# Softmax denominators divided once per batch, and a step table for each engine, in a transformer block on one core

## What is computed

```python
x = layernorm(x + attn(x))
logits = x @ router_w + router_b
probs = softmax(logits); top_p, top_i = top_k(probs, 2); top_p /= top_p.sum(-1)
h = silu(x @ w1[e]) * (x @ w3[e])          # for each expert e
x = layernorm(x + sum_e gates[:, e] * (h @ w2[e]))
```

## Time and profile before

| | us |
|---|---|
| median of three runs | 432.3 |
| profiled execution | 429.85 |
| its span | 428.1 |
| TensorE busy in the span | 374.9 (88%) |
| VectorE busy | 327.2 (76%) |
| ScalarE busy | 246.9 (58%) |
| GpSimd busy | 205.8 (48%) |
| a steady attention stage, 174.5 to 199.0 | 24.5 |
| end of attention, first expert matmul | 247.64 |
| last matmul | 421.68 |

### The profile page before, as it was taken

One profiled execution on the slowest core, in us unless ns is written; L12 is line 12 of the kernel. 1 busy time (PEld: TensorE's weight loads), 2 busy tenths in 40 slices (PEclk: granted clock), 3 DMA queues, 4 the chain that ended last, 5 costly groups with the idle time before them and its releaser, 6 DMA issues.

```text
span 428.1 us, 7151 instructions
## 1 busy us (share of the span) xinstructions
PE 374.9 (88%) x2276; PEld 190.4 (44%) x2298; DVE 327.2 (76%) x973; ACT 246.9 (58%) x347; POOL 205.8 (48%) x267
## 2 busy tenths in 40 slices
PE   7879799997999999999997896888878889789993
PEld 3432222322233232323223265676657666567881
DVE  4878998997999999998995526656884687565655
ACT  2454177776878787877875853454345434445560
POOL 6067688515244251434433143545464555446771
PEclk9996889999999999999998998999999999999997
DMA  6762014483332433243011040000200020003000
GB/s 224 232 174 48 1 23 100 144 260 59 91 83 47 103 76 93 52 112 57 11 17 25 3 125 0 0 0 3 98 24 2 0 100 26 0 1 100 25 1 25
DMA packets 49635, 27.44 MB, mean 64 GB/s; under 512 B 31227, under 2 KB 45243, under 8 KB 49598
## 3 DMA queue, kind: packets, MB, share of 16 engines
q1 hardware_dynamic: 46702, 25.09, 22.5%
q10 hardware_dynamic: 2896, 1.90, 1.5%
HBM read 17.31 MB, written 7.38 MB: 58 GB/s over the span
## 4 chain that ended last, share of the span: by engine, by line
PE 52%; DVE 20%; issue 12%; ACT 6%; POOL 6%; DMA 2%; ACTq 0%; POOLq 0%; DVEq 0%; SPq 0%
PE o_bank L1254 12%; PE bank L1213 9%; PE t_bank L1236 7%; PE bank L1318 6%; PE t_bank L1318 5%; PE t_bank L1331 5%; PE small_bank L1213 4%; POOL hid_lo L680 4%; DVE maxima L962 3%; DVE den_all L1018 3%; DVE num L1090 3%; DVE x_tw L958 3%; ACT num L836 3%; ACT num L777 2%; DVE mg_t L958 2%
## 5 line engine op out<-in xcount | busy, mean ns | idle before, releaser
L777 ACT ACTIVATE num<-t_bank 128x1024 f32<-128x1024 f32 (+2 forms) x160 | 141.9, 943 | 61.8 <-PE t_bank L1236 61.7
L680 POOL TENSOR_TENSOR hid_lo<-num,q_op 128x512 fp32r<-128x512 f32 x63 | 86.2, 1373 | 67.7 <-ACT q_op L829 67.1
L650 POOL TENSOR_SCALAR_AFFINE_SELECT num<-num 128x512 f32<-128x512 f32 x64 | 40.2, 638 | 96.0 <-ACT num L777 94.4
L1254 PE MATMUL o_bank<-num,v_op 128*32 128x512 f32 (+3 forms) x768 | 79.6, 501 | 0.9
L829 ACT ACTIVATE q_op<-num 128x512 fp32r<-128x512 f32 x64 | 40.4, 632 | 65.0 <-DVE num L1090 64.3
L1213 PE MATMUL bank<-k_op,q_op 128*128 128x512 bf16 (+7 forms) x232 | 67.2, 338 | 2.5 <-DVE maxima L958 1.2
L962 DVE TENSOR_REDUCE maxima<-bank 128x1 f32<-128x512 f32 x90 | 59.8, 685 | 3.1 <-PE bank L1213 2.7
L1236 PE MATMUL t_bank<-q_op,k_op 64*128 64x512 bf16 (+3 forms) x384 | 49.4, 334 | 4.9 <-DMA q_op<-max_rows 2.2
L1090 DVE TENSOR_TENSOR num<-bank,num 128x512 f32<-128x512 f32 x32 | 22.1, 691 | 38.7 <-ACT num L836 32.4
L1213 PEld LDWEIGHTS bank<-k_op,q_op 128*128 128x128 bf16 x254 | 21.0, 97 | 57.9 <-DVE maxima L958 20.0
L958 DVE CUSTOM_DVE_ANT_0 x_tw<-bank,resid 128x256 f32<-128x256 f32 (+7 forms) x100 | 43.2, 454 | 4.4 <-PE bank L1213 3.5
(11 more groups left out here) (150 smaller groups left out, 604.6 us busy)
## 6 DMA issues: line engine op xcount, KB each, us to landing
q_op<-q_scratch SPq DMA_DIRECT2D x64, 48.0 KB
k_op<-k_scratch SPq DMA_DIRECT2D x32, 96.0 KB, 2.3
w_raw<-in_w_all SPq DMA_DIRECT2D x6, 512.0 KB, 4.6
turns_sb<-gate_scratch SPq DMA_DIRECT2D x8, 256.0 KB, 3.7
num<-gate_scratch SPq DMA_DIRECT2D x8, 256.0 KB, 3.8
xT<-o_sb SPq DMA_DIRECT2D x32, 32.0 KB
den_all<-o_sb SPq DMA_DIRECT2D x32, 32.0 KB
x_res<-in_x_tok ACTq DMA_DIRECT2D x4, 256.0 KB, 3.0
```

The costliest lines, as they stand in the source:

```text
L650: pool.affine_select(out=tile, in_=tile, compare_op=ALU.is_ge, fill=0.0, base=0, pattern=[[0, GH], [1, P]], channel_multiplier=-1)\
L680: pool.tensor_tensor(hid_lo[:, m % HB, :], hid[:, m % HB, :], hid_hi[:, m % HB, :].bitcast(F32), ALU.subtract).then_inc(f_lo, 1)
L777: act.activation(num[:, t % PB, :, off:CH].rearrange("p (k i) t -> p i k t", i=2)[:, :, h:h + each, :], t_bank[k % TB][:, :, 0:each * (CH ...
L1254: ins = pe.matmul(o_bank[h * QD:(h + 1) * QD, off:CH], v_op[w][:, kt, h, :], num[:, t % PB, h, off:CH], start=kt == 0, stop=kt == TI * (c ...
```

## The change

**Denominators.** Of the eight equal rows of a head only one is taken, and it goes to memory: `gather_heads` issues four transfers of sums and one of four rows of `o_sb`, [4 x 1024], to `den_scratch`. When a batch's four groups are there, `load_den` loads its 16 x 1024 denominators as a tile of 128 x 128, VectorE takes the reciprocal in place (`turn_den`), `store_rden` stores it, and `spread_rden` loads it into `rden_all` with each head's row in eight partitions. For batch 0 these stand, on SP, in the stage of group 5 (load, behind the weights and the gathering), in the last steady stage (store behind the gathering, spread at its end), and on VectorE at the head of the last steady stage; for batch 1 on SP behind the last gathering, and on VectorE behind unit 9 of chunk 0. Front step r = 0 is the product alone. ScalarE's copy of a group waits for the transfers of two groups before, and now for the denominators' too.

**Steps.** The rule r + 3 gives way to a table per engine. Before, r stood at step r + 3 everywhere; after:

| engine | r: step |
|---|---|
| TensorE | 1: 3, 6: 10, 8: 13, 14: 18 |
| VectorE | 0: 1, 1: 3, 2: 4, 3: 5, 5: 8, 7: 11, 9: 13, 10: 14, 11: 15, 13: 17, 14: 18 |
| ScalarE | 7: 11, 8: 12, 12: 16 |
| GpSimd | 3: 6 |

(TensorE's matmuls of r = 1 stood at step 4 before, since its work for the front steps has its own numbers: 1, 6, 8, 14.) The gates' product of an expert and its sum, both in unit 6 + 4e before, stand in units 6 + 4e and 7 + 4e. The transposes behind the last unit move from step 19 to 21, the statistics from 20 to 21 and 22 in halves, the variance from 21 to 23, 1/sqrt to 24, the output from 22 to 25. ScalarE does a unit's copies and Silus first, those of the older chunk behind those of the newer, and a front step last.

```diff
-TR_STEP = EO_STEP + UNITS - FT + 1
-STAT_STEP = TR_STEP + 1
-VAR_STEP = RSTD_STEP = STAT_STEP + 1
-Z_STEP = VAR_STEP + 1
+TR_STEP = EO_STEP + UNITS - FT + 3
+STAT_STEP = TR_STEP
+VAR_STEP = STAT_STEP + 2
+RSTD_STEP = VAR_STEP + 1
+Z_STEP = RSTD_STEP + 1
+RDEN_STEP = 9
...
-NEXT_AT = E_LAST
-def next_steps(n, i):
-    r = n - NEXT_AT
-    return [(i + 1 + r // UNITS, r % UNITS)] if i + 1 + r // UNITS < CHUNKS else []
+PE_NEXT = {1: 3, 6: 10, 8: 13, 14: 18}
+DVE_NEXT = {0: 1, 1: 3, 2: 4, 3: 5, 5: 8, 7: 11, 9: 13, 10: 14, 11: 15, 13: 17, 14: 18}
+ACT_NEXT = {7: 11, 8: 12, 12: 16}
+POOL_NEXT = {3: 6}
+def next_steps(n, i, table):
+    at = i * UNITS + n
+    return [(ch, r) for ch in range(1, CHUNKS) for r, step in table.items() if (ch - 1) * UNITS + step == at]
...
                 for h in range(GH):
-                    for k, dst in enumerate((o_all, den_all)):
-                        at, rows = g * QD + h * DH, h * QD + k * DH
-                        sp.dma_start(dst[at:at + DH, b * S:(b + 1) * S], o_sb[n % 2][rows:rows + DH, :])\
-                            .then_inc(heads_in[b][n % 2], 16)
+                    at = g * QD + h * DH
+                    sp.dma_start(o_all[at:at + DH, b * S:(b + 1) * S], o_sb[n % 2][h * QD:h * QD + DH, :])\
+                        .then_inc(heads_in[b][n % 2], 16)
+                sp.dma_start(den_dram[b, g * GH:(g + 1) * GH, :], o_sb[n % 2][DH:P:QD, :])\
+                    .then_inc(den_stored[b][n % 2], 16)
+            def load_den(b):
+                for i in range(2):
+                    sp.wait_ge(den_stored[b][i], 16 * (NG // 2))
+                sp.dma_start(den_sb[:, b, :], den_dram[b, :, :].rearrange("h (k t) -> (h k) t", t=P))\
+                    .then_inc(den_loaded[b], 16)
+            def store_rden(b):
+                sp.wait_ge(den_turned[b], 1)
+                sp.dma_start(rden_dram[b, :, :].rearrange("h (k t) -> (h k) t", t=P), den_sb[:, b, :])\
+                    .then_inc(rden_stored[b], 16)
+            def spread_rden(b):
+                sp.wait_ge(rden_stored[b], 16)
+                sp.dma_start(rden_all[:, b * S:(b + 1) * S], rden_dram[b, :, :].unsqueeze(1).broadcast_to([H, DH, S]))\
+                    .then_inc(rden_loaded[b], 16)
...
                         if step == ("T", 1, TI, 0, 0):
                             gather_heads(n - 1)
+                            if s == GROUPS - 1:
+                                store_rden(0)
+                        if step == ("END",) and s == GROUPS - 1:
+                            spread_rden(0)
...
+                        if n == NG + 1:
+                            load_den(0)
...
                 if ch == 0:
                     gather_heads(GROUPS - 1)
+                    load_den(B - 1)
+                    store_rden(B - 1)
+                    spread_rden(B - 1)
...
+                            act.wait_ge(den_stored[(g - 2) // NG][g % 2], 16 * ((g - 2) % NG // 2 + 1))
...
-                steps = next_steps(n, i)
-                for ch, r in steps:
-                    if r == 1:
-                        between(ch, ch // NC, ch % NC, r)
-                experts_hi(i, n)
                 if n >= UNITS:
                     experts_hi(i + 1, n - UNITS)
-                for ch, r in steps:
-                    if r != 1:
-                        between(ch, ch // NC, ch % NC, r)
+                experts_hi(i, n)
                 experts_silu(i, n)
                 if n >= UNITS:
                     experts_silu(i + 1, n - UNITS)
+                for ch, r in next_steps(n, i, ACT_NEXT):
+                    between(ch, ch // NC, ch % NC, r)
...
+            def turn_den(b):
+                dve.wait_ge(den_loaded[b], 16)
+                dve.reciprocal(den_sb[:, b, :], den_sb[:, b, :]).then_inc(den_turned[b], 1)
...
-                    dve.reciprocal(den_all[:, at], den_all[:, at]).then_inc(c_mg, 1)
-                    dve.wait_ge(c_mg, ch + 1)
-                    dve.tensor_tensor(mg_t[:, :], o_all[:, at], den_all[:, at], ALU.mult).then_inc(c_mgs, 1)
+                    dve.tensor_tensor(mg_t[:, :], o_all[:, at], rden_all[:, at], ALU.mult).then_inc(c_mgs, 1)
...
+                if n > EO_STEP and (n - EO_STEP) % FT == 1 and n < EO_STEP + 1 + UNITS:
+                    e = (n - EO_STEP) // FT
                     for k, half in enumerate(halves(ch, e)):
                         dve.wait_ge(f_eo, 2 + ch * E + e + 1 + k)
...
-                if n == STAT_STEP:
-                    for i in range(TI):
+                if n in (STAT_STEP, STAT_STEP + 1):
+                    for i in range(TI // 2 * (n - STAT_STEP), TI // 2 * (n - STAT_STEP + 1)):
...
+                if (ch, n) == (0, RDEN_STEP):
+                    turn_den(B - 1)
```

More of the change, by code:

```diff
@@ L367, in transformer_block @@
         heads_in = [[sem(f"heads_in{b}{i}") for i in range(2)] for b in range(B)]
+        den_stored = [[sem(f"den_stored{b}{i}") for i in range(2)] for b in range(B)]
+        den_loaded, den_turned, rden_stored, rden_loaded = ([sem(f"{n}{b}") for b in range(B)] for n in (
+            "den_loaded", "den_turned", "rden_stored", "rden_loaded"))
         max_split, max_joined, split_step, ident_cast = sem("max_split"), sem("max_joined"), sem("split_step"), sem("ident_cast")
@@ L688, in _ @@
                 experts(0, n)
-                for step in next_steps(n, 0):
+                for step in next_steps(n, 0, POOL_NEXT):
                     between(*step)
@@ L695, in _ @@
                     experts(i, n)
-                    for step in next_steps(n, i):
+                    for step in next_steps(n, i, POOL_NEXT):
                         between(*step)
@@ L979, in stage @@
                         experts(0, step[1])
+                        for next_step in next_steps(step[1], 0, DVE_NEXT):
+                            between(*next_step)
             for s in range(GROUPS):
@@ L1133, in _ @@
                 experts(0, n)
-                for step in next_steps(n, 0):
+                for step in next_steps(n, 0, DVE_NEXT):
                     between(*step)
@@ L1140, in _ @@
                     experts(i, n)
-                    for step in next_steps(n, i):
+                    for step in next_steps(n, i, DVE_NEXT):
                         between(*step)
@@ L1350, in _ @@
                 experts(0, n)
-                for step in next_steps(n, 0):
+                for step in next_steps(n, 0, PE_NEXT):
                     between(*step)
@@ L1357, in _ @@
                     experts(i, n)
-                    for step in next_steps(n, i):
+                    for step in next_steps(n, i, PE_NEXT):
                         between(*step)
```

13 lines of the change are left out of this document (9 added, 4 removed).

## The result

The changed kernel takes 401.2 us in the median of four runs (401.1 to 402.81), the kernel before 432.28 (431.94 to 432.59) beside it. The ratio is 0.929, interval 0.9265 to 0.9314: faster, and inside the range. The profiled execution of after took 401.1 us with a span of 399.4, where before had 429.85 and 428.1. So 28.7 us of span have to be found.

What follows compares the result with a forecast made beforehand. TensorE should be full but waits 7.7 us per chunk for VectorE's work or a ScalarE copy. 3.0 + 9.8 + 17.8 - 0.4 - 0.3 = 29.9 us off 429.85 gives 399.95, median 402.4 us, range 397.5 to 412.

Steps and rivals of the forecast that it cites:

- Sum: Whole kernel: savings of 29.9 us off the profiled 429.85 us give 399.95, and a median of 402.4 us.
- The 2.45: Whole kernel: the median was taken to lie 2.45 us above the profiled run.
- part 3: Last attention stage: wait of 1.62 us for mg_t goes, plus 0.75 and some 0.8 of slow clock; 3.0 us, bounds 1.6 to 3.4.
- Part 1: Divisions on VectorE: 128x128 per batch at 0.85 us instead of 3.34 us per chunk; the second costs nothing.
- The 0.3 of loss: Last steady stage: the first division, beyond 0.64 us of VectorE idle time, may push the score ring; bounds 0 and 0.9.
- Part 2: Denominators through memory: spread lands between 221 and 224.5, hidden with 1 to 3 us of cover; at the far end costs 1 us.
- SP is freed by 2 us per group: SP's queue: each group issues five transfers instead of eight at 0.7 us each.
- Part 4: Expert chunks: the table spreads VectorE's work; waits at small pieces go, stops cost 0.5 us per chunk, bounds 0 and 2.
- L999 1.3 to 3.0: Step 8 of a chunk on VectorE: four x1 operations take 1.3 to 3.0 us together beside GpSimd's remainders.
- Rival (a): Expert chunks: the shared lock holds VectorE's sums, 1.3 us more in four steps, 9 us in three chunks, 411 us; chance 0.10.
- Rival (b): Expert chunks: waits move, the projection waiting for gates_t behind the router; only the divisions' share is left, 421 us; chance 0.12.
- Rival (c): Attention stages: ScalarE's copies wait for the denominators' store if it takes over 30 us; 33 us lost, 435; chance 0.03.

Runs made afterwards that it cites:

- e3: Changed kernel with three extra SP transfers behind the denominators of group 0 (402.47 us) or of each of groups 1 to 7 (401.18 us).
- after_again: The changed kernel itself, untouched, timed once more on another chip: 399.43 us, ratio 0.9256 to the kernel before.
- e5_again: Changed kernel with the steps from x1's transposes through the router one unit earlier, timed a second time: 397.5 us, ratio 0.9212 to the kernel before.
- e2: Changed kernel with the new step table but the old denominators (eight transfers per group, division of 512 columns in each chunk): 416.35 us, ratio 0.9613 to before.
- e1: Kernel before with the denominators' path through memory and one division per batch, steps as before: 422.77 us, ratio 0.9765 to before.

## Why the prediction was right, step by step

- **Sum.** 29.9 us were forecast off the profiled run, 28.7 came (399.95 against 401.1), and the median then lay 0.1 above the profiled run, not 2.45. Two misses of 1.2 and 2.35 with opposite signs give 402.4 against 401.2; that part of the closeness is luck. The 2.45 may have been the clock's: where before was timed again, the mean granted clock of an execution lay between 0.956 and 0.973 and its time between 435.68 and 428.45, longer mostly where the clock was lower. After's four runs all had 0.972. And the range's low end doesn't add up as stated: 3.4 in part 3, no stops and no loss give 397.75 from the 399.95 of the profiled run, but 400.2 from the forecast of 402.4.
- **Part 1, divisions at 0.85 us.** L979 took 0.95 at 195.78 and 0.94 in chunk 0, and the idle time of 0.64 behind the first is gone. The score ring lost nothing: the starts of the mask part in that stage and the one before (172.89, 197.43) lie 24.54 us apart, as in before. The 0.3 of loss came all the same, 0.29 in the next stage (24.94 against 24.65), but by GpSimd's cast that VectorE's product held, which the forecast didn't have. The size is right by luck.
- **Part 2, path through memory.** The spread left SP at 213.57 and the page gives 4.4 us to landing, so 218.0, earlier than 221; mg_t was made at 220.62 and nobody waited. Right, with more cover than stated. "SP is freed by 2 us per group" was right as a size and wrong as a price: it was 2.2 us at group 0. The step that failed is that I looked for who stood behind the three new transfers and not for who stood behind the three removed. e3 shows it.
- **Part 3, last attention stage 3.0 us.** The 1.62 came. The 0.75 and 0.8 of the slow clock didn't: I read "after that idle time" as a cause, from one trace. after_again and e5_again, equal in code and idle time, show that the idle time before it doesn't decide it. In after_again, without the stretch, A is 5.06 shorter than before's: 2.2 early and 2.8 here, near my 3.0. So whether part 3 comes out is a matter of the execution. In after A shrank by 3.93, 2.2 of it early and 1.7 here, below my 3.0 and just above my lower bound of 1.6. In 1.7, the 0.29 of part 1 is taken off.
- **Part 4, chunks.** 9.8 + 17.8 - 0.4 = 27.2 forecast, 8.88 + 7.65 + 8.18 = 24.7 measured. The mechanism was right, and no wait is left at the four small pieces. Mis-sized was the full chunk, 36.25 against 37.53. The stop took 1.27 and not 0.5: 0.75 of idle time and 0.5 by which the units before and behind it are slower, which a row of idle time doesn't show. The other 0.5 is small work: the unit behind each small piece takes 2.16 (304.48 to 306.64) and not 2.07, and the one transpose of gates 0.26 behind a stop (283.59 to 285.92 is 2.33), 0.08 without one, where I had 0.1.
- **"L999 1.3 to 3.0."** The four x1 operations of a chunk took 1.10 us and were not held by a remainder. Instead small operations of the router got 1.2 to 1.4 us each, which the forecast knew from one row, the 1.27 of L1063. The lateness landed in step 15, as forecast, with other owners.
- **Rival (a)**, the lock on the sums, didn't come: sums took 0.68 to 0.80 us. The lock turned on VectorE all the same, on operations of 16 to 64 columns, for 1.27 us a chunk instead of 3. **Rival (b)**'s wait before the projection came where the division stayed, in e2, and not in after. **Rival (c)**: nothing waited for the store.

## What to carry to other kernels

When a queue is made shorter, look for the transfer with the least time behind each removed entry, as one does for an added one; three transfers of 21 more mattered here. A table of steps pays even where one operation is longer than the slack between two of the repeated ones (14.9 us with the division of 3.3 us in place), but each such operation leaves a stop, here 3.07 us. Before you call two parts of a change dependent, compare the granted clock of the traces: some 5 of the 6 us that seemed to come only from both were slow stretches and not waits. On VectorE beside a busy GpSimd, count a tiny operation with two SBUF inputs at the length of GpSimd's operation, 1.2 to 1.4 us here, and look the other way too, at what VectorE holds up on GpSimd.

## What the runs showed of the hardware

- Operations of 128x16 to 128x64 on VectorE take 0.2 to 0.5 us, and 1.16, 1.23 and 1.36 when a remainder of GpSimd of 1.3 us has begun just before; they end within 0.1 us of it. One of 128x4 with a single SBUF input took 1.14 instead of 0.17. A cast of 128x16 on GpSimd took 0.48 instead of 0.20 when a product of 128x512 on VectorE had begun 0.3 us before.
- The granted clock of one stretch fell to 0.50 in one run and stayed at 1.00 in another with equal code and equal idle time before it (0.99 us). Within one trace (e2) a stop of 3.07 us was followed by 0.50 and one of 3.08 was not. A matmul of 128x512 takes 0.63 us at 0.50 and 0.39 at 1.00. Between two projections e1, with a wait of 1.78 us less than before and a slow stretch more, took 45.15 us against 45.17.
- A transfer of eight rows out of `o_sb` costs SP 0.62 to 0.71 us of queue (once 1.54), the packed store of four denominator rows 0.51, and eight against five of them moved a chain 2.9 us.
- A matmul of 128x512 behind a small one takes 0.47 to 0.50 us instead of 0.39, and its unit 2.16 instead of 2.07. A stop of 0.75 us costs 1.27 to 1.32 by the starts around it.
